# Layer 2's attention output comes out with features on partitions, P is divided before its turns, and layer 0's weights are split in two parts

## The chip, the cores and the metric

The kernel runs on one core of one Trainium2 chip. The metric is the time of the whole program on the device, in microseconds (us). The time before is the median of 3 runs.

## The reference

x is [128 graphs, 64 nodes, 256 features], adj one 64x64 matrix of zeros and ones. Four layers follow each other, each as x = layernorm(x + layer(x)):

- Layer 0, graph attention: h = x W; s1 = h a1 and s2 = h a2 (two columns); e = leaky_relu(s1_i + s2_j) * adj; att = softmax(e); elu(att h + beta h).
- Layer 1: (adj x) W + bias.
- Layer 2, attention with 8 heads of 32: softmax(q k^T / sqrt(32)), masked by adj, times v; then o W_proj + b_proj, and o + layernorm(o) with gamma and beta.
- Layer 3, three gated steps: a = adj h; r = sigmoid(a w4 + h u3), z = sigmoid(a w3 + h u3), hv = tanh(a w5 + (r h) u5), h = (1 - z) h + z hv.

## The kernel before

The 8192 rows are cut into 16 units of 512 rows (8 graphs), in four tiles of 128 rows, two graphs each. Products with weights are taken in three passes of TensorE (L122 to L124): the high part of both operands, and each high with the other's low part. So every operand is copied once by ScalarE (high part, L1440) and once by VectorE (low part, L2217). A "gate group" of layer 3 is six such matmuls with 512 columns.

The layers of different units are interleaved. The body of the loop, i = 1 to 11, holds layer 3 of unit i, layer 2's attention of unit i+1, layer 1 and layer 2's projections of unit i+2, and layer 0 of unit i+3. Around the loop are a fill (units 0 to 2 begin) and a drain. Each engine has its own program: a written list of calls in `body`, `fill` and `drain` (TensorE from L924, ScalarE from L1618, VectorE from L2521), and semaphores order them. Every list is carried out strictly in the order written. SyncE issues the loads of x, the stores, and the swap of V's halves; POOL computes the inverse roots of the normalizations. PSUM is two sets of four banks, X and Y: in the loop layer 3 works in X, and layers 0, 1 and 2 in Y (`front`); for unit 0 `front` is X.

Layer 2's attention of a unit goes so: `l2_mask` and `l2_score` (TensorE) write scores for 4 tiles and 8 heads; VectorE takes the row maximum (`l2_max`, L2367) and subtracts it into `prob` (`l2_shift`, L2377); ScalarE takes exp (`l2_exp`, L1527), not yet divided. TensorE turns P by 16 transposes (`l2_turn_prob`, L797), ScalarE copies the result (`l2_take_prob`). `l2_attend` (L812) is 64 matmuls with the turned P stationary and, as moving operand, 64 columns of V and two columns of ones, so that the row sums of P come out beside the output. VectorE takes the reciprocals of the sums (`l2_inverse`, L2383), adds NaN for rows without a neighbour (`l2_nan`), and multiplies the output by them into `o_tok` (`l2_share`, L2395). The rows are then on partitions, so eight transposes (`l2_turn_o`, through `turn`, L646) bring the features there; `l2_high_o` and `l2_low_o` copy them, and `l2_output` multiplies with W_proj.

In the fill, layer 0's W and its two columns W a1 and W a2 are one matrix of 258 columns. VectorE computes the columns (`sum_a`, four operations), ScalarE takes the high part of all 258 (`high_l0`), VectorE the low part (`low_l0`), and `l0_project` (258 columns for each tile) waits for it. `l0_diagonal` (VectorE), `l0_spread` (TensorE, L698), the softmax on VectorE and ScalarE, `l0_turn_att` (L706) and `l0_attend` (L714) follow. `keep_busy` issues transposes of the identity whose result nobody reads: 38 in the fill.

## Time and profile before

| | |
|---|---|
| median of 3 runs | 1385.81 us (1384.9 to 1387.71) |
| the profiled execution, whole | 1390.11 us |
| its span, first to last instruction | 1388.3 us |
| mean granted TensorE clock | 0.987 |
| instructions | 26972 |
| busy: VectorE / ScalarE / POOL | 1057.0 / 783.7 / 134.2 us |
| the chain that ended last | TensorE 91%, VectorE 6%, ScalarE 2%, issue 1% |

How to read it: a busy share is a mean over the span. Matmuls are pipelined, so that the duration of one (some 400 ns for 512 columns) is longer than the distance to the next (some 235 ns); distances between starts are what counts. PEclk is the granted clock of TensorE, 1.00 for 2.4 GHz and 0.50 for 1.2 GHz; between them a stretch holds both.

### The profile page before, as it was taken

How to read it: one execution, taken by the hardware profiler on the slowest of the kernel's cores; microseconds unless marked ns; L12 is line 12 of the kernel's file. 1: busy time of each engine (PE TensorE's matmuls, PEld its weight loads, DVE VectorE, ACT ScalarE, POOL GpSimd, SP SyncE). 2: the span in 40 equal slices, each digit the busy share in tenths (PEclk: the TensorE clock that was granted, in tenths of full speed). 3: DMA queues.
4: the chain of work that ended last, by engine and by line, in shares of the span. 5: the costliest groups of instructions: out<-in, count | busy, mean ns of one | idle time of the engine just before them, and what ended most of it. 6: DMA issues, size and time to landing. Idle time of an engine off the chain costs nothing.

```text
span 1388.3 us, 26972 instructions
## 1 busy us (share of the span) xinstructions
PE 1345.8 (97%) x10447; PEld 1143.7 (82%) x10447; DVE 1057.0 (76%) x2371; ACT 783.7 (56%) x1449; POOL 134.2 (10%) x194
## 2 busy tenths in 40 slices
PE   7879999999999999999999999999999999999996
PEld 6768888888888888888888888888888888887785
DVE  5776878877787887778787787887778877868465
ACT  3536556656465565656646565664656556564453
POOL 4000101000010100100000010100001010010000
PEclk8979999999999999999999999999999999999998
DMA  5001010000000000000000000000000000010000
GB/s 176 9 1 39 1 24 32 17 13 25 23 30 23 30 15 8 30 23 30 23 30 8 15 30 23 30 15 23 15 23 30 23 31 1 9 38 20 27 1 30
DMA packets 54670, 34.53 MB, mean 25 GB/s; under 512 B 34912, under 2 KB 51552, under 8 KB 54624
## 3 DMA queue, kind: packets, MB, share of 16 engines
q1 hardware_dynamic: 52816, 29.43, 7.1%
q0 software_dynamic: 1248, 3.94, 0.9%
q8 instruction: 31, 0.51, 0.1%
q10 hardware_dynamic: 560, 0.52, 0.1%
q14 instruction: 15, 0.12, 0.0%
HBM read 12.92 MB, written 8.39 MB: 15 GB/s over the span
## 4 chain that ended last, share of the span: by engine, by line
PE 91%; DVE 6%; ACT 2%; issue 1%; DMA 0%; POOL 0%; POOLq 0%; DVEq 0%; ACTq 0%
PE banks L122 22%; PE banks L124 21%; PE banks L123 21%; PE banks L651 8%; PE banks L646 4%; PE banks L812 2%; PE banks L714 2%; PE banks L797 2%; PE banks L914 2%; PE banks L786 2%; PE banks L698 1%; PE banks L775 1%; PE banks L706 1%; DVE l_s L2243 0%; DVE late_lo L2217 0%
## 5 line engine op out<-in xcount | busy, mean ns | idle before, releaser
L1574 ACT ACTIVATE l_r<-banks,bias_r 128x512 f32<-128x512 f32 x90 | 61.5, 683 | 182.3 <-PE banks L124 182.3
L1591 ACT ACTIVATE banks<-banks,bias_h 128x512 f32<-128x512 f32 x96 | 63.5, 662 | 107.0 <-PE banks L124 106.5
L262 POOL TENSOR_TENSOR l_rstd<-l_mv,eps 128x4 f32<-128x4 f32 x47 | 18.3, 389 | 877.2 <-DVE l_mv L256 877.2
L2217 DVE TENSOR_TENSOR l_rh_lo<-l_r,l_rh_hi 128x512 fp32r<-128x512 f32 x90 | 60.7, 687 | 52.9 <-ACT l_rh_hi L1440 51.7
L276 ACT ACTIVATE y<-l_sum,l_offset,l_rstd 128x256 f32<-128x256 f32 x128 | 71.1, 595 | 11.8 <-DVE l_offset L270 11.8
L122 PE MATMUL banks<-l_rh_hi,u_hi 128*128 128x512 f32 x180 | 75.2, 418 | 0.7 <-DVE l_rh_lo L2217 0.7
L1440 ACT ACTIVATE l_rh_hi<-l_r 128x512 fp32r<-128x512 f32 x90 | 54.0, 630 | 36.5 <-DVE l_r L2460 36.5
L1585 ACT ACTIVATE banks<-banks,bias_z 128x512 f32<-128x512 f32 x96 | 62.9, 656 | 17.7 <-PE banks L124 17.7
L124 PE MATMUL banks<-l_rh_lo,u_hi 128*128 128x512 f32 x180 | 71.1, 395 | 0.0
L123 PE MATMUL banks<-l_rh_hi,u_lo 128*128 128x512 f32 x180 | 70.8, 394 | 0.0
L651 PE MATMUL banks<-adj_t,y 128*128 128x128 f32 x544 | 69.5, 277 | 0.5 <-ACT y L276 0.2
L651 PEld LDWEIGHTS banks<-adj_t,y 128*128 128x128 f32 x544 | 64.6, 192 | 4.1 <-issue 3.2
L2478 DVE SCALAR_TENSOR_TENSOR l_r<-banks,l_r 128x512 f32<-128x512 f32 x90 | 61.6, 686 | 5.3 <-ACT banks L1585 2.0
L651 PE MATMUL banks<-adj_t,l_htok 128*128 128x128 f32 x480 | 62.6, 278 | 0.1
L651 PEld LDWEIGHTS banks<-adj_t,l_htok 128*128 128x128 f32 x480 | 57.3, 192 | 6.0 <-ACT l_htok L1440 5.3
L2460 DVE SCALAR_TENSOR_TENSOR l_r<-l_r,l_h 128x512 f32<-128x512 f32 x60 | 40.9, 682 | 26.7 <-ACT l_r L1574 26.7
L1507 ACT ACTIVATE l_qk<-banks 128x512 f32<-128x512 f32 x64 | 38.3, 600 | 40.3 <-PE banks L124 39.8
L2471 DVE TENSOR_TENSOR l_r<-banks,l_h 128x512 f32<-128x512 f32 x60 | 41.1, 685 | 23.4 <-ACT banks L1591 23.3
L2217 DVE TENSOR_TENSOR l_h_lo<-l_h,l_h_hi 128x512 fp32r<-128x512 f32 x60 | 40.9, 682 | 18.1 <-ACT l_h_hi L1440 18.0
L122 PE MATMUL banks<-late_hi,qkv_hi 128*128 128x512 f32 x128 | 51.8, 404 | 2.4 <-DVE late_lo L2217 2.4
L2367 DVE TENSOR_REDUCE l_mx<-banks 128x8 f32<-128x512 f32 x64 | 42.3, 682 | 14.8 <-PE banks L786 14.8
L124 PE MATMUL banks<-late_lo,qkv_hi 128*128 128x512 f32 x128 | 51.6, 403 | 0.0
(304 smaller groups left out, 4331.9 us busy)
## 6 DMA issues: line engine op xcount, KB each, us to landing
x_tok<-in_x_dram SPq DMA_DIRECT2D x15, 512.0 KB, 3.5
l_res<-y SPq DMA_DIRECT2D x15, 512.0 KB, 3.0
out_dram<-l_res SPq DMA_DIRECT2D x15, 512.0 KB, 3.0
l_vpair<-l_vstage SPq DMA_DIRECT2D x32, 128.0 KB, 3.2
w_raw<-in_L_gnn_w_w_dram POOLq DMA_DIRECT2D x3, 512.0 KB, 7.7
qkv_raw<-in_L_gnn_w_qkv_dram POOLq DMA_DIRECT2D x1, 768.0 KB, 4.4
l_res<-in_x_dram SPq DMA_DIRECT2D x1, 512.0 KB, 5.1
u_raw<-in_L_gnn_u_w_dram POOLq DMA_DIRECT2D x2, 256.0 KB, 7.7
```

Of the source, the lines that this page charges most:

```text
L122: nc.tensor.matmul(out, w[0], x[0], start=first, stop=False, skip_group_check=True)
L123: nc.tensor.matmul(out, w[1], x[0], start=False, stop=False, skip_group_check=True)
L124: return nc.tensor.matmul(out, w[0], x[1], start=False, stop=last, skip_group_check=True)
L276: return self.p.nc.scalar.activation(y[:, t, :], z[:, t, :], ACT.Identity, scale=self.rstd[:, t:t + 1], bias=self.offset[:, t:t + 1])
L646: ins = nc.tensor.transpose(bank[:, columns(t)], tokens[:, t, k * P:(k + 1) * P], p.ident[:, :])
L651: ins = nc.tensor.matmul(bank[:, columns(t)], tokens[:, t, k * P:(k + 1) * P], p.adj_t[:, :], start=True, stop=True)
L1440: return nc.scalar.activation(out, source, ACT.Copy)
L1574: nc.scalar.activation(own(u).r[:, m, :], rz(u)[:, m, :], ACT.Tanh, scale=0.5, bias=w.biases["r"][:, m:m + 1]).then_inc(s.r_ready.of(u), 1)
L1585: nc.scalar.activation(rz(u)[:, m, :], rz(u)[:, m, :], ACT.Tanh, scale=0.5, bias=w.biases["z"][:, m:m + 1]).then_inc(s.z_ready.of(u), 1)
L1591: nc.scalar.activation(hv(u)[:, m, :], hv(u)[:, m, :], ACT.Tanh, bias=w.biases["h"][:, m:m + 1]).then_inc(s.hv_ready.of(u), 1)
L2217: return nc.vector.tensor_tensor(parts[1][:, k, :], bank, parts[0][:, k, :].bitcast(F32), ALU.subtract)
L2478: nc.vector.scalar_tensor_tensor(own(u).r[:, m, :], rz(u)[:, m, :], 1.0, own(u).r[:, m, :], ALU.add, ALU.mult).then_inc(s.step.of(u), 1)
```

## The change

Layer 2. VectorE now sums P's rows with four reductions (`l2_sum`), takes the reciprocals and adds NaN as before, and multiplies P by them in place (`l2_normal`), four operations, before the turns; `l2_turn_prob` waits for that. `l2_attend` has its operands exchanged: V is stationary, the turned P moves, and the output has features on partitions, in the layout that `l2_high_o` reads. `l2_turn_o`, `l2_share` and the ones columns are gone (VW is 64 instead of 66).

```diff
         def l2_turn_prob(u, t):
-            pe.wait_ge(*s.l2_exp.at(u, t + 1))
+            pe.wait_ge(*s.l2_prob_shared.at(u, t + 1))
...
         def l2_attend(u, t):
-            pe.wait_ge(*s.l2_prob_t.at(u, t + 1))
-            for g in range(HP):
+            pe.wait_ge(*s.l2_prob_t.at(u, max(t + 1, CH)))
+            for c in range(CH):
                 for n in range(PER_TILE):
-                    at = g * P + n * NODES
-                    ins = nc.tensor.matmul(front(u)[n * NODES:(n + 1) * NODES, t, g * VW:(g + 1) * VW],
-                                           probt[:, t, at:at + NODES], b.v_pair[:, n, t, g, :],
-                                           start=True, stop=True)
+                    for g in range(HP // CH):
+                        at = (c * (HP // CH) + g) * P + n * NODES
+                        ins = nc.tensor.matmul(front(u)[g * VW:(g + 1) * VW, c, t * P + n * NODES:t * P + (n + 1) * NODES],
+                                               b.v_pair[:, n, t, c * (HP // CH) + g, :], probt[:, t, at:at + NODES],
+                                               start=True, stop=True)
...
-        def l2_turn_o(u, k):
-            if k == 0:
-                pe.wait_ge(*s.l2_o.at(u, 1))
-            turn(front(u)[:, k, :], b.o_tok, k).then_inc(s.l2_o_turned.sem, 1)
...
         def l2_high_o(u, k):
-            act.wait_ge(*s.l2_o_turned.at(u, k + 1))
+            act.wait_ge(*s.l2_pv_done.at(u, TILES))
...
+        def l2_sum(u, t):
+            dve.wait_ge(*s.l2_exp.at(u, t + 1))
+            nc.vector.tensor_reduce(b.inv[:, t, :], b.prob[:, t, :, :], AX.X, ALU.add).then_inc(s.l2_inv.sem, 1)
...
+        def l2_normal(u, t):
             if t == 0:
-                dve.wait_ge(*s.l2_inv.at(u, 2))
-            ins = nc.vector.tensor_tensor(b.o_tok[:, t, :].rearrange("p (g e d) -> p g e d", g=HP, e=2),
-                                          heads(u)[:, t, :, 0:2 * HD].rearrange("p g (e d) -> p g e d", e=2),
-                                          b.inv[:, t, :, :].unsqueeze(3).to_broadcast([P, HP, 2, HD]), ALU.mult)
+                dve.wait_ge(*s.l2_inv.at(u, TILES + 2))
+            nc.vector.tensor_tensor(b.prob[:, t, :, :], b.prob[:, t, :, :],
+                                    b.inv[:, t, :].unsqueeze(2).to_broadcast([P, HEADS, NODES]),
+                                    ALU.mult).then_inc(s.l2_prob_shared.sem, 1)
```

Layer 0's weights. W's 256 columns are split by themselves as soon as W has landed; the two s columns are split after `sum_a` (`high_columns`, `low_columns`). For unit 0 the s columns are multiplied separately, 24 matmuls of two columns (`project_columns`), ahead of the projections, and copied by VectorE (`take_columns`). The spread of unit 0 goes to another bank, after the first projection.

```diff
         def high_l0():
+            act.wait_ge(w.loaded[0], 16)
+            nc.scalar.activation(w.l0[0][:, :, 0:DIM], w.l0_raw[:, :, 0:DIM], ACT.Copy).then_inc(ws["l0_hi"], 1)
+
+        def high_columns():
             act.wait_ge(ws["start_chain"], SUMS_OF_A)
-            nc.scalar.activation(w.l0[0][:, :, :], w.l0_raw[:, :, :], ACT.Copy).then_inc(ws["l0_hi"], 1)
+            nc.scalar.activation(w.l0[0][:, :, DIM:WX], w.l0_raw[:, :, DIM:WX], ACT.Copy).then_inc(ws["columns_hi"], 1)
...
+        def project_columns():
+
+            pe.wait_ge(ws["columns_ready"], 1)
+            pe.wait_ge(*s.l0_lo.at(0, CH))
+            for t in range(TILES):
+                ins = rows_by_weights(s_columns[:, t, :], b.early, t, w.l0, slice(DIM, WX))
+            ins.then_inc(ws["l0_columns"], 1)
```

Unit 0's three first normalizations are applied half by ScalarE (tiles 0, 1) and half by VectorE (tiles 2, 3). The orders of all engines are rewritten. In the loop's body TensorE's order between the scores and the output, where calls that are the same on both sides stand once, is now:

```diff
             l2_mask(i + 1)
-            l3_w(i, 0, 0)
             l2_score(i + 1, 0)
...
             l3_u(i, 0, 0)
             l3_u(i, 0, 1)
             l3_r(i, 0, 0)
+            l3_w(i, 0, 0)
+            l3_w(i, 0, 1)
             l3_r(i, 0, 1)
-            l3_w(i, 0, 1)
+            l3_diff(i, 0, 0)
             l2_turn_prob(i + 1, 0)
...
             l2_attend(i + 1, 3)
-            l3_diff(i, 0, 0)
             l3_candidate(i, 0, 0)
-            l2_turn_o(i + 1, 0)
-            l2_turn_o(i + 1, 1)
             l3_candidate(i, 0, 1)
             l3_diff(i, 0, 1)
             l2_output(i + 1, 0)
```

And VectorE's there:

```diff
             l2_shift(i + 1, 3)
+            l3_variance(i - 1)
             l3_reset(i, 0, 0)
+            l2_sum(i + 1, 0)
+            l2_sum(i + 1, 1)
+            l2_sum(i + 1, 2)
+            l2_sum(i + 1, 3)
+            l2_inverse(i + 1)
+            l3_offset(i - 1)
+            l2_nan(i + 1)
+            l2_normal(i + 1, 0)
+            l2_normal(i + 1, 1)
+            l2_normal(i + 1, 2)
+            l2_normal(i + 1, 3)
             l3_reset(i, 0, 1)
-            l3_variance(i - 1)
             l3_low_rh(i, 0, 0)
             l3_low_rh(i, 0, 1)
-            l2_inverse(i + 1)
-            l2_nan(i + 1)
-            l2_share(i + 1, 0)
-            l2_share(i + 1, 1)
-            l2_share(i + 1, 2)
-            l2_share(i + 1, 3)
+            l2_low_o(i + 1, 0)
             l3_difference(i, 0, 0)
-            l2_low_o(i + 1, 0)
```

On ScalarE the fourth exponential now stands ahead of the second reset, and the second r*h copy ahead of the fourth copy of P. In the fill `keep_busy` has 159 transposes at 16 places instead of 38 at four; the projections of unit 2 stand ahead of unit 0's turns of P. In the drain layer 3's `l3_diff` stands earlier.

## Rows read from the trace of the kernel before

**Rows 1.** The page, part 1: busy time, share of the span, instructions.
```profile
PE 1345.8 (97%) x10447; PEld 1143.7 (82%) x10447; DVE 1057.0 (76%) x2371; ACT 783.7 (56%) x1449; POOL 134.2 (10%) x194
```

**Rows 2.** Windows: stretch, its length, busy time of each engine, PEclk, DMA share.
```profile
12.40:17.00 4.60, 4.52 (x24) 4.44 (x24) 2.13 (x15) 1.16 (x3) 4.60 (x7) 0.63 0.94 195
24.90:30.60 5.70, 5.62 (x20) 4.91 (x21) 3.25 (x5) 2.93 (x5) 0.00 (x0) 0.55 0.01 3
71.00:80.40 9.40, 6.84 (x92) 6.23 (x90) 6.41 (x19) 5.33 (x10) 1.21 (x2) 0.82 0.01 2
85.00:105.00 20.00, 14.31 (x56) 11.11 (x56) 17.49 (x48) 6.03 (x12) 2.46 (x4) 0.66 0.00 1
0.00:105.00 105.00, 80.88 (x648) 70.22 (x649) 73.72 (x184) 44.33 (x84) 23.12 (x44) 0.87 0.20 62
...
544.50:626.80 82.30, 82.21 (x647) 70.09 (x647) 65.02 (x146) 48.37 (x90) 7.45 (x10) 1.00 0.07 22
1250.00:1388.30 138.30, 122.91 (x676) 101.05 (x674) 86.65 (x179) 63.40 (x110) 7.50 (x12) 0.96 0.05 20
```

**Rows 3.** Timeline of TensorE in one loop turn: start, duration, instruction.
```profile
612.95 0.50 PE L122 MATMUL banks<-f_h_hi,u_hi 128*128 128x512 f32 x1
...
620.06 1.91 PE L797 MATMUL banks<-ident,l_prob 128*128 128x128 f32 x16
621.90 2.10 PE L812 MATMUL banks<-l_vpair,l_qk 128*64 128x66 f32 x64
623.92 0.50 PE L122 MATMUL banks<-f_a_hi,diff_hi 128*128 128x512 f32 x1
...
626.83 1.03 PE L646 MATMUL banks<-ident,l_otok 128*128 128x128 f32 x8
627.62 0.47 PE L122 MATMUL banks<-l_rh_hi,u_hi 128*128 128x512 f32 x1
...
628.39 0.39 PE L122 MATMUL banks<-l_rh_hi,u_hi 128*128 128x512 f32 x1
...
629.08 0.39 PE L122 MATMUL banks<-f_a_hi,diff_hi 128*128 128x512 f32 x1
```

**Rows 4.** Groups of VectorE: count, busy us and mean ns, idle before.
```profile
L2367 DVE TENSOR_REDUCE l_mx<-banks 128x8 f32<-128x512 f32 x64 | 42.3, 682 | 14.8 <-PE banks L786 14.8
L2377 DVE TENSOR_TENSOR l_prob<-banks,l_mx 128x512 f32<-128x512 f32 x64 | 42.0, 679 | 0.1
...
L2395 DVE TENSOR_TENSOR l_otok<-banks,l_inv 128x256 f32<-128x256 f32 x64 | 22.7, 416 | 0.5
...
L2383 DVE RECIPROCAL l_inv<-banks 128x32 f32<-128x32 f32 x16 | 5.6, 352 | 7.0 <-PE banks L812 7.0
```

**Rows 5.** Timeline of VectorE in the same loop turn.
```profile
613.01 1.29 DVE L2367 TENSOR_REDUCE l_mx<-banks 128x8 f32<-128x512 f32 x2 [1.22 <-PE banks L786]
...
616.61 1.27 DVE L2377 TENSOR_TENSOR l_prob<-banks,l_mx 128x512 f32<-128x512 f32 x2
```

**Rows 6.** Timeline of ScalarE in the same loop turn.
```profile
617.46 0.69 ACT L1574 ACTIVATE l_r<-banks,bias_r 128x512 f32<-128x512 f32 x1 [8.33 <-PE banks L124]
618.04 1.66 ACT L1527 ACTIVATE l_prob<-l_prob 128x512 f32<-128x512 f32 x3
```

**Rows 7.** Timeline of TensorE in the fill; in brackets the idle time before and its releaser.
```profile
12.48 0.39 PE L122 MATMUL banks<-l_w_hi,early_hi 128*128 128x258 f32 x1 [1.97 <-DVE l_w_lo L2157]
...
18.15 0.67 PE L698 MATMUL banks<-l_s,same_graph 128*128 128x256 f32 x2 [1.03 <-DVE l_s L2243]
...
24.98 3.78 PE L714 MATMUL banks<-l_h,l_att_t 128*128 128x256 f32 x8 [0.69 <-ACT l_att_t L1440]
...
38.27 2.05 PE L651 MATMUL banks<-adj_t,y 128*128 128x128 f32 x16 [0.22 <-ACT y L276]
...
115.99 0.47 PE L122 MATMUL banks<-f_h_hi,u_hi 128*128 128x512 f32 x1
```

**Rows 8.** Timeline of TensorE in the drain.
```profile
1290.45 1.09 PE L914 MATMUL banks<-ident,l_h 128*128 128x128 f32 x8 [2.30 <-DVE l_h L2484]
```

1552 lines of the change are left out of this document (801 added, 751 removed).

## The prediction

> **What bounds the kernel now.** I read the page first: TensorE is busy for 97% of the span, VectorE for 76% [rows 1]. A mean hides stages, so I took windows. One turn of the loop lasts 82.3 us and TensorE is busy for 82.21 of them at full clock, VectorE for 65.02; the first 105 us are another regime, with 24.1 us in which TensorE does nothing (105.0 - 80.88) and a mean granted clock of 0.87; the last 138.3 us hold 15.4 us of idleness [rows 2]. So in the loop a TensorE instruction that goes is time that goes, unless a new wait takes its place, and VectorE has 17 us of air per unit. In the fill what counts is the chain of hand-overs, and whether the clock is at 2.4 or 1.2 GHz when the work comes. In four stretches of it the clock stands at 0.63, 0.55, 0.82 and 0.66; busy time by missing clock is 4.52 x 0.37 + 5.62 x 0.45 + 6.84 x 0.18 + 14.31 x 0.34 = 10.3 us that the same columns would not need at full clock [rows 2].
>
> The sum is made against the profiled execution, 1390.1 us with a span of 1388.3. It is 4.3 us above the median of 1385.8; I take the difference found onto the median.
>
> **1. The output's turns go.** Eight 128x128 transposes a unit. In the loop they start at 626.83 and the next matmul at 627.62, 0.79 us; the three passes after it take 0.77 instead of the 0.69 of the next ones, which is the price of going back from these small transposes to the long matmuls [rows 3]. 0.79 + 0.07 = 0.86 us a unit, all of it on the engine that bounds, 16 units: -13.8 us. In the fill, where TensorE also idles, part of this is only air; I count that in step 5.
>
> **2. The attention matmuls with operands swapped.** 64 a unit, before and after. Before, P is stationary and V moves in 66 columns (the two ones columns give the row sums); after, V is stationary and P moves in 64. They take from 621.90 to 623.92, 2.02 us [rows 3], 32 ns each. If streaming sets the pace, 2 of 66 columns are 0.06 us a unit; if loading 64 stationary columns does, nothing. Consecutive instructions still go to alternate halves of the columns. Between 0 and -1.0 us for 16 units; I take -0.5, the middle. The Trainium skill (TensorEngine Tiling (Array Packing), Key Properties) says that changing the tiling mode drains TensorE; both versions switch into and out of this mode once a unit, so the 0.07 us above stays paid here and the rule changes nothing but the warning that splitting blocks costs.
>
> **3. More switches.** The new body splits two blocks of small matmuls (layer 1's second aggregation, layer 2's second input turn) and joins one (mask and scores): about half a switch more per unit, between 0 and 0.15 us each way. I take +0.04 a unit, +0.6 us in all.
>
> **4. VectorE ahead of P's turns.** It gets four row sums over 128x512 and four multiplications of 128x512, and loses four 128x256 shares. Nearest rows: the row maximum (a reduction of the same size, from PSUM) 682 ns, the subtraction in P 679, share 416, reciprocal 352, and the NaN add, which is no longer than that [rows 4]. In sequence they start every 0.6 us (two maxima take 1.29 together [rows 5]). So VectorE gets 8 x 0.6 - 4 x 0.36 = 3.4 us a unit, 65 to 68.4 of some 81: it fits by throughput. Neither operation is seen with both ends in SBUF; bounds 0.5 and 0.9 us each.
>
> By latency: let 0 be the start of the first l3_u after the scores, 612.95. Before, the path to P's turns was: four maxima, four shifts (end 617.88, 4.93), ScalarE's reset from 617.46 (4.51), four exponentials at 5.09, 5.61, 6.13 and (now without the reset between) 6.65 [rows 5, 6]; TensorE reached the turns at 620.06, 7.11, after five gate groups of 1.41 us [rows 3]. The new order puts seven groups there: 9.95. VectorE in the new order: shifts to 4.9, layer 3's variance 0.4, reset 5.2 to 5.9, sums at 5.9, 6.5, 7.1, 7.7 (the last waits for the last exponential, done 7.3), reciprocal 8.4, NaN add 8.8, multiplications from 9.05 every 0.6, ending 9.7, 10.3, 10.9, 11.5. TensorE's four groups of turns (0.46 each, 1.84 from 620.06 to 621.90) are there at 9.95, 10.41, 10.87, 11.33. The last is late by 0.2 us. The first attention group now waits for two copies of P, and ScalarE does layer 3's second r*h copy before the last P copy; by the same addition that copy ends near 13.6 and its group is due at 13.7. Candidate 0 needs both low parts of r*h, ready at 13.8 against 14.2. Then 4.2 us of candidates and gates lie over o's high and low copies (2 x 0.6 + 0.7, with a tanh between them). So the cover just holds everywhere. A stall of 0.2 us by this addition; with each of the eight new operations 0.1 longer than the 0.6 it is 1.0. I take 0.24 a unit for the 14 units from the loop on: +3.3 us. Layer 3's second r*h is queued behind the multiplications; it is the next to be late.
>
> A rule speaks against the change: the Trainium skill (VectorE: DVE Perf Modes, Rules for kernel authors) calls tensor_reduce the slowest VectorE operation and says to restructure where it is on a hot path, and here sums that came from ones columns become reductions. The trace does not bear it out for this size: the maximum takes 682 ns and a tensor_tensor 679 [rows 4]. By that rule alone the sums would be late, which is case D below.
>
> **5. The fill.** Before, four sum operations and a split of the whole W stand ahead of the first projection, which starts at 12.48 after 1.97 us idle, and the spread of s2 waits for all four projections, copies and diagonal: 18.15 [rows 7]. After, W's 256 columns are split at once and the two s columns by themselves: 24 matmuls of two columns before the projections, 0.7 to 2.4 us (24 x 0.032 of step 2, or x 0.10 of the turns), I take 1.5; the diagonal follows without the 4.5 us of projections at half speed. Spread at about 14, 4 us earlier. The first attend (3.78 us for 8 matmuls at half clock, 24.98 [rows 7]) takes half of that if the clock is kept. Half of the tiles of unit 0's three normalizations go to VectorE, which shortens each by some 1.0 us (two of four ScalarE applications); that is on the chain that ends at 38.27 with the first aggregation [rows 7]. Against it: unit 0's P is now divided with no layer 3 to cover it, 8 x 0.6 + 0.6 - 1.4 (shares) = 4.0 us; four projections of unit 2 (2.9 us) are moved over it. The filler transposes rise from 38 to 159, 121 more by 0.10 = 12 us of TensorE time; they cost nothing while they lie in the 24 us of idleness, and all of the 12 if that idleness has gone. Their use is the 10.3 us of missing clock. Sum: at best -4 - 3 - 10.3 + 2 = about -15; at worst the clock is not kept and fillers get in the way, +4. I take -8, nearer to the best end, since I can follow the chain to the spread and to the first attend and these alone give -6. POOL now sums the biases before unit 0's root, so that root waits for the last weight load; that is hidden unless the loads end later than that root is due, 6 us before its old place at the earliest. The issues on SP (unit 3's x before the keeping of y2 of unit 0) have no taker near.
>
> **6. The drain.** Its orders are new. The 2.30 us wait for h before a turn at 1290 [rows 8] should shrink, as the gates are issued earlier; unit 15's division has gates over it. Between -3 and +3; I take 0.
>
> Sum: -13.8 - 0.5 + 0.6 + 3.3 - 8 = -18.4 us: 1371.7 of the profiled execution, 1367.4 on the median; I say **1367**.
>
> **Cases.**
> A (0.58). As summed, 1367, its own range 1361 to 1374.
> B (0.12). No stall in the loop and the fill at its best end: 1367.4 - 3.3 - 5 = 1359. For it: the loop before has 0.1 us of idleness in 82, and the new order gives exactly two more gate groups as cover.
> C (0.15). The fill gives nothing because its chain, not TensorE, sets the pace and the fillers only fill: 1375. For it: in 85 to 105 us VectorE is busy for 17.49 of 20 [rows 2]. Against: the clock there is 0.66.
> D (0.08). Eight new operations at 0.7 or the sums late: stall 1.0 a unit, 14 - 3.3 = 11 more: 1378.
> E (0.07), slower. P's turns wait fully: if sums and multiplications run after the last exponential and layer 3's reset and r*h queue between them, the last multiplication ends near 14 instead of 11.5, a stall of 2.6 us at every unit: 1367.4 - 3.3 + 14 x 2.6 = 1400. It decides from a stall of (18.4 + 3.3) / 14 = 1.55 us a unit. Against it: the order interleaves the sums with the exponentials.
> That the change does not do what it says would show in 128 transposes still there; the diff leaves no caller, I give it nothing.
>
> 0.2% or 2.8 us is what a measurement tells from no change. Faster: all of A, B, C, D less a rest, 0.90; same 0.03; slower 0.07. The range runs from B's to just above D's time, 1357 to 1380; C and D are each at the other end of a cost that I could only bound.
>
> **What would show it.** Right: no group of transposes on the output tile; the loop's period 81.4 to 81.7 instead of 82.3; idle before P's turns, put down to VectorE's multiplication, under 0.3 us in each loop turn; the multiplication and the sum at 0.6 to 0.7 us; the spread near 14, the first l3_u of unit 0 at 106 to 109 instead of 115.99 [rows 7], and a granted clock above 0.95 in the first 105 us. Wrong: a period of 82.3 or more (step 4), the clock still near 0.87 (step 5), or waits of the u5 matmuls for r*h's low part in each loop turn.

## The result and the profile after

| | before | after |
|---|---|---|
| median beside each other on one chip | 1387.44 us (8 runs) | 1381.68 us (8 runs) |
| ratio | | 0.9958, 95% interval 0.9945 to 0.9971 |
| the profiled execution, its span | 1388.3 us | 1380.3 us |

The change makes the kernel faster by 0.42%, 5.8 us, and by 8.0 us between the two profiled executions. 18.4 were forecast. 1381.7 lies above the range of 1357 to 1380.

The page, part 1, of the kernel after, against [rows 1]:

```profile
PE 1350.2 (98%) x10464; PEld 1143.7 (83%) x10464; DVE 1109.4 (80%) x2441; ACT 796.3 (58%) x1444; POOL 138.2 (10%) x194
```

128 transposes are gone, 121 idle ones and 24 matmuls of two columns have come (17 instructions more), and TensorE is busy for 4.4 us longer: a matmul that waits in the middle of its group is shown as busy. A busy sum doesn't answer the question. The windows, against [rows 2], say a little more (length, PE, PEld, DVE, ACT, POOL, clock, DMA):

```profile
0.00:105.00 105.00, 95.93 (x850) 87.19 (x850) 81.92 (x202) 49.55 (x95) 25.39 (x44) 0.97 0.24 73
...
544.50:626.80 82.30, 82.17 (x643) 69.46 (x642) 68.45 (x152) 50.12 (x92) 7.63 (x10) 1.00 0.07 22
1250.00:1380.30 130.30, 115.00 (x629) 94.97 (x627) 80.02 (x166) 58.48 (x102) 7.29 (x12) 0.95 0.06 21
```

In the first 105 us the granted clock went from 0.87 to 0.97, as step 5 wanted. In the loop VectorE has 3.4 us more of work, as step 4 had it.

What does answer it is a mark that every unit passes. The mask of a unit is the first matmul of its attention; here are the masks of units 1, 2, 3 and 13 and the last group of TensorE. Before:

```profile
113.71 0.61 PE L775 MATMUL banks<-mask_bias,ident_bf 64*128 64x512 bf16 x4
...
197.07 0.61 PE L775 MATMUL banks<-mask_bias,ident_bf 64*128 64x512 bf16 x4
...
280.15 0.61 PE L775 MATMUL banks<-mask_bias,ident_bf 64*128 64x512 bf16 x4
...
1102.72 0.61 PE L775 MATMUL banks<-mask_bias,ident_bf 64*128 64x512 bf16 x4
...
1377.38 1.14 PE L914 MATMUL banks<-ident,x_tok 128*128 128x128 f32 x8 [2.20 <-DVE x_tok L2484]
```

After:

```profile
103.50 0.60 PE L804 MATMUL banks<-mask_bias,ident_bf 64*128 64x512 bf16 x4
...
187.82 0.61 PE L804 MATMUL banks<-mask_bias,ident_bf 64*128 64x512 bf16 x4
...
273.33 0.83 PE L804 MATMUL banks<-mask_bias,ident_bf 64*128 64x512 bf16 x4
...
1094.10 0.61 PE L804 MATMUL banks<-mask_bias,ident_bf 64*128 64x512 bf16 x4
...
1369.93 1.48 PE L937 MATMUL banks<-ident,x_tok 128*128 128x128 f32 x8 [2.32 <-DVE x_tok L2524]
```

After minus before: -10.2, -9.2, -6.8, -8.6, -7.4 us. So the fill (all that lies ahead of the loop) gives all that it was to give (unit 1), 3.4 us are lost again between units 1 and 3 (1.0 up to unit 2, in the last part of the fill, and 2.4 behind it), ten turns of the loop give 1.8 together, 0.18 each, and the drain takes 1.2. The period is (1094.10 - 273.33) / 10 = 82.08 us, against 82.26; 81.4 to 81.7 was forecast.

**One loop turn.** TensorE, against [rows 3]:

```profile
613.39 0.40 PE L124 MATMUL banks<-f_a_lo,diff_hi 128*128 128x512 f32 x1
613.62 2.46 PE L826 MATMUL banks<-ident,l_prob 128*128 128x128 f32 x16
616.01 2.08 PE L841 MATMUL banks<-l_qk,l_vpair 128*64 128x64 f32 x64
618.03 0.50 PE L122 MATMUL banks<-l_rh_hi,u_hi 128*128 128x512 f32 x1
```

P's turns took 1.84 us from their first start to the start of the attend, and take 2.39 in this turn (2.34 in the mean); no idle time stands before them, because TensorE waits between the groups of four, inside the row. VectorE in the same turn:

```profile
606.45 2.47 DVE L2413 TENSOR_TENSOR l_prob<-banks,l_mx 128x512 f32<-128x512 f32 x4
...
609.14 0.65 DVE L2500 SCALAR_TENSOR_TENSOR l_r<-l_r,f_h 128x512 f32<-128x512 f32 x1
609.72 2.46 DVE L2419 TENSOR_REDUCE l_inv<-l_prob 128x8 f32<-128x512 f32 x4
612.21 0.35 DVE L2424 RECIPROCAL l_inv<-l_inv 128x32 f32<-128x32 f32 x1
612.48 0.10 DVE L272 SCALAR_TENSOR_TENSOR l_offset<-l_mv,l_rstd 128x4 f32<-128x4 f32 x1
612.60 0.24 DVE L2430 TENSOR_SCALAR l_inv<-l_inv,nan_rows 128x32 f32<-128x32 f32 x1
612.87 2.50 DVE L2437 TENSOR_TENSOR l_prob<-l_prob,l_inv 128x512 f32<-128x512 f32 x4
```

The first multiplication ends at about 613.5, just when TensorE is through with its gates, and the other three follow at 0.6 us. TensorE needs 0.46 for a group, so it runs at VectorE's pace: its groups of four start at 613.62, 614.22, 614.82 and 615.43. The groups of VectorE, against [rows 4]:

```profile
L2413 DVE TENSOR_TENSOR l_prob<-banks,l_mx 128x512 f32<-128x512 f32 x64 | 40.0, 678 | 0.0
L2437 DVE TENSOR_TENSOR l_prob<-l_prob,l_inv 128x512 f32<-128x512 f32 x64 | 40.0, 686 | 0.5
L2419 DVE TENSOR_REDUCE l_inv<-l_prob 128x8 f32<-128x512 f32 x64 | 39.7, 675 | 0.4 <-ACT l_prob L1558 0.2
```

The new operations cost 675 and 686 ns, within the bounds of 0.5 and 0.9, and the sum is no slower than the subtraction.

**The loop's entry.** TensorE at unit 2, in the first turn of the loop:

```profile
187.82 0.61 PE L804 MATMUL banks<-mask_bias,ident_bf 64*128 64x512 bf16 x4
188.36 1.56 PE L815 MATMUL banks<-l_qk 32*64 32x64 f32 x125
191.67 0.33 PE L815 MATMUL banks<-l_qk 32*64 32x64 f32 x3 [1.75 <-issue]
...
193.44 0.63 PE L124 MATMUL banks<-f_h_lo,u_hi 128*128 128x512 f32 x1
193.87 0.63 PE L122 MATMUL banks<-f_h_hi,u_hi 128*128 128x512 f32 x1
```

Three matmuls from its end, the block of 128 short score matmuls stands still for 1.75 us, and nothing that the profile shows is waited for ("issue"). A microsecond later matmuls come every 0.43 us instead of 0.235 for some 3.4 us: the granted clock there is 0.50, 1.2 GHz. Before, the same block stood still for 0.51 us and the clock stayed at 1.00. 1.75 - 0.51 plus seven distances longer by 0.196 is 2.6 us, which covers the 2.4 lost between the masks of units 2 and 3.

**The same fill in six traces.** There is a second trace of the kernel after (e15 below), and e5, e6, e7 and e9 have its fill and change the loop alone. In these six traces the mask of unit 1 comes at 101.8 to 102.0 us where the clock stays at 1.00 in the first 105 us (e5, e6, e15) and at 103.5 to 103.8 where it falls for 3.4 or 6.8 us (after, e7, e9). A difference of 2 us at unit 1 between single traces can so be the clock of one execution and nothing of the kernel.

### The profile page after: what moved, and what is told of

Its sections match the earlier page's. It is cut to its first block, busy times and chain, and to the rows that moved or that the text cites. A ratio compares the mean times of both kernels' runs of the same rounds, so it can differ in the third digit from the quotient of the medians.

```text
span 1380.3 us, 27146 instructions
## 1 busy us (share of the span) xinstructions
PE 1350.2 (98%) x10464; PEld 1143.7 (83%) x10464; DVE 1109.4 (80%) x2441; ACT 796.3 (58%) x1444; POOL 138.2 (10%) x194
## 4 chain that ended last, share of the span: by engine, by line
PE 91%; DVE 5%; ACT 2%; issue 1%; DMA 0%; POOL 0%; SPq 0%; POOLq 0%; ACTq 0%; DVEq 0%
PE banks L122 23%; PE banks L124 22%; PE banks L123 22%; PE banks L667 9%; PE banks L662 3%; PE banks L937 2%; PE banks L826 2%; PE banks L841 2%; PE banks L743 2%; PE banks L815 2%; PE banks L725 1%; PE banks L804 1%; PE banks L656 1%; PE banks L735 0%; DVE early_lo L2249 0%
## 5 line engine op out<-in xcount | busy, mean ns | idle before, releaser
L2249 DVE TENSOR_TENSOR early_lo<-banks,early_hi 128x512 fp32r<-128x512 f32 x62 | 41.8, 685 | 36.1 <-ACT early_hi L1469 35.8
L278 ACT ACTIVATE y<-l_sum,l_offset,l_rstd 128x256 f32<-128x256 f32 x124 | 68.2, 593 | 2.8 <-DVE l_offset L272 2.7
L1469 ACT ACTIVATE late_hi<-banks 128x512 fp32r<-128x512 f32 x66 | 39.1, 597 | 38.6 <-PE banks L662 23.1
```

The lines of the kernel that those rows point to most:

```text
L278: return self.p.nc.scalar.activation(y[:, t, :], z[:, t, :], ACT.Identity, scale=self.rstd[:, t:t + 1], bias=self.offset[:, t:t + 1])
L1469: return nc.scalar.activation(out, source, ACT.Copy)
L2249: return nc.vector.tensor_tensor(parts[1][:, k, :], bank, parts[0][:, k, :].bitcast(F32), ALU.subtract)
```

## The experiments

"Before" ran beside each set: 1387.0, 1387.7, 1386.9, 1387.6 and 1386.1 us, for e1 to e4, e5 to e8, e9 and e10, e11 to e13, and e14 and e15.

### VectorE's pace: less work for it (e1)

This kernel leaves the row sums out, so that P is divided by 1.

```diff
-            nc.vector.tensor_reduce(b.inv[:, t, :], b.prob[:, t, :, :], AX.X, ALU.add).then_inc(s.l2_inv.sem, 1)
+            nc.vector.memset(b.inv[:, t, :], 1.0).then_inc(s.l2_inv.sem, 1)
```

> The changed kernel with the four row sums per unit (2.46 us of VectorE) replaced by four small memsets, so P is divided by 1: the division's chain is some 2.2 us shorter and nothing else changes. Theory V (VectorE's pace in the chain sums, reciprocal, NaN, multiplications sets when P's turns end): the block of 16 turns falls from 2.34 us back to 1.84 as before the change, the loop's period from 82.08 to about 81.55, the time by 11 x 0.5 plus 1 to 2 us in fill and drain, to about 1375. Rival T (the turns cost more on TensorE itself, because each group now waits by itself or because of the stretch around it): block and period stay, the time stays within 1.5 us of 1381.7. The drain's wait for h of unit 14 (3.7 us) should shrink only if VectorE's load for unit 15 makes it: about 2.4 us less VectorE work ahead of it, so 1.3 to 2.4 us under that theory, unchanged if it is the chain of layer 3 itself.

Measured: 1376.15 us, ratio 0.9923 (0.9902 to 0.9945). TensorE in the same turn:

```profile
612.12 1.91 PE L826 MATMUL banks<-ident,l_prob 128*128 128x128 f32 x16
613.99 2.09 PE L841 MATMUL banks<-l_qk,l_vpair 128*64 128x64 f32 x64
```

The turns are back at 1.87 us in every loop turn, and the period is 81.70 us against 82.08. Nothing of TensorE was changed, so what stretched them is VectorE's lateness, worth 0.38 us a turn, and 5.1 to 5.5 us of the kernel (10.9 us under its "before" where the kernel after is 5.8 under its own; 1376.15 against 1381.68). The stall at the entry (1.90 us) and the drain's wait for h (3.6 us) stayed: they have other causes.

### The fourth multiplication on POOL (e3)

```diff
+            nc.gpsimd.tensor_tensor(b.prob[:, t, :, :], b.prob[:, t, :, :],
+                                    b.inv[:, t, :].unsqueeze(2).to_broadcast([P, HEADS, NODES]),
+                                    ALU.mult).then_inc(s.l2_last_shared.sem, 1)      # t = TILES - 1, POOL's list
```

> The changed kernel with the fourth of the four multiplications of P moved from VectorE to POOL, beside the other three. VectorE's chain gets 0.6 us shorter. Theory V: if POOL's multiplication of 128x512 takes up to 2.0 us, it ends when the last turn needs it, the block of turns falls from 2.34 to about 1.9, the period to about 81.65, the time to about 1376. If it takes over 2.5 us, the fourth group of turns waits for it and the block grows by what it is over: at 4 us some 2 us a unit, 1405. Rival T: with a POOL time under 2 us nothing moves. No row so far shows a POOL operation of this size but a memset of 0.53 us; tensor_tensor of 4 elements takes 0.33 to 0.55.

Measured: 1389.97 us, ratio 1.0026 (1.0012 to 1.0040), period 82.77. The groups, VectorE and then POOL:

```profile
L2457 DVE TENSOR_TENSOR l_prob<-l_prob,l_inv 128x512 f32<-128x512 f32 x48 | 44.0, 967 | 0.5
...
L593 POOL TENSOR_TENSOR l_prob<-l_prob,l_inv 128x512 f32<-128x512 f32 x16 | 24.7, 1542 | 93.5 <-DVE l_inv L2448 93.5
```

The mean of 967 ns mixes two sizes. VectorE's three and POOL's one in the same turn:

```profile
614.23 0.69 DVE L2457 TENSOR_TENSOR l_prob<-l_prob,l_inv 128x512 f32<-128x512 f32 x1
614.84 1.53 DVE L2457 TENSOR_TENSOR l_prob<-l_prob,l_inv 128x512 f32<-128x512 f32 x1
616.29 0.68 DVE L2457 TENSOR_TENSOR l_prob<-l_prob,l_inv 128x512 f32<-128x512 f32 x1
...
614.27 1.55 POOL L593 TENSOR_TENSOR l_prob<-l_prob,l_inv 128x512 f32<-128x512 f32 x1 [1.98 <-DVE l_inv L2448]
```

One of the three, in every unit, takes 1.53 us and the other two keep their 0.69 and 0.68; the long one begins while POOL's is under way and ends after it. Together they take 2.74 us, more than four at 0.6, and the second group of turns waits for the long one (0.80 us). The help costs more than it saves. The Trainium skill (SBUF — State Buffer, Who interferes with whom) says that a VectorE instruction with two inputs in SBUF contends with a GpSimd instruction that reads SBUF. The trace agrees, with 0.84 us on one VectorE instruction in each unit and nothing on the others.

### The fill: idle transposes, halves, order

```diff
e2: keep_busy 12, 5, 3 and 18 at the places of the kernel before, the other groups out (159 -> 38)
e4: unit 0's three normalizations, t = 2 and 3: VectorE's calls out, ScalarE's loops over range(4)
e10, TensorE's fill:
-            project_columns()
             l0_turn(1, 1)
...
-            l0_spread(0)
             for n in range(1, 4):
                 l0_project(0, n)
+            project_columns()
+            l0_spread(0)
```

> The changed kernel with the filler transposes of the fill cut from 159 to 38, at the places where the old kernel had them (12, 5, 3, 18). Theory K (the fill's gain of 10 us is to a good part kept clock): the mean granted clock of the first 105 us falls from 0.97 towards the old 0.87, the mask of unit 1 comes 4 to 7 us later, and the time goes up by as much, to 1386 to 1389. Rival C (the gain is the shorter chain alone, fillers only fill idleness): the clock falls but the mask of unit 1 moves by less than 1.5 us and the time stays within 1.5 us of 1381.7. Rival W (fillers are in the way): 2 to 4 us faster.

> The changed kernel with unit 0's three normalizations applied by ScalarE alone again (four tiles each), VectorE's three pairs taken out. If these applications are on the fill's chain, each of the three ends some 1.0 us later and the mask of unit 1 comes 2 to 3 us later, the time goes up by 2 to 3 us to 1384 to 1385. Rival: other work covers them, the time stays within 1 us.

> The changed kernel with the attention's two columns of unit 0 (project_columns) and l0_spread(0) behind the four projections of unit 0 in TensorE's fill, as in the kernel before, and not ahead of them; the weights stay in two parts. It prices the order that the weights in two parts allow. Theory K2 (it is the head of the fill's chain): VectorE's scores of unit 0, which begin at 17.5 in the changed kernel, begin 3 us later, the mask of unit 0 comes 2.5 to 3 us later, that of unit 1 too, and the end 2 to 3: 1384. Rival (the fill's chain goes through the loads and the weights of the layers behind, so the head's 3 us are absorbed by the waits between): masks of units 0 and 1 within 1 us, and 1382.

| | median, ratio | mask of unit 1 | unit 2 | unit 3 |
|---|---|---|---|---|
| after | 1381.68, 0.9958 | 103.50 | 187.82 | 273.33 |
| e2 | 1382.85, 0.9970 (0.9955 to 0.9985) | 106.83 | 192.04 | 273.92 |
| e4 | 1383.59, 0.9979 (0.9965 to 0.9993) | 106.35 | 190.15 | 274.06 |
| e10 | 1383.75, 0.9981 (0.9969 to 0.9993) | 105.12 | 189.51 | 273.19 |

Without its part unit 1 comes later by 3.3 us (e2), 2.9 (e4) and 1.6 (e10). By the scatter of 2 us between traces of the same fill, e2 and e4 are clear of it, and e10 isn't: what the order of the columns is worth is not shown. Theory K wanted 4 to 7 us for the idle transposes and is near with 3.3; the halves were priced at 2 to 3 and came so. At unit 3 all stand within 0.9 us of each other, and the whole times differ by 1 to 2 us, hardly more than the intervals. It looks as if the entry took whatever the fill gained, but the traces say otherwise: from unit 2 to unit 3 the kernel after needs 85.5 us, e4 83.9 and e10 83.7, each with a stall in unit 2's scores (1.75, 1.75 and 1.46 us) and only the first with a fall of the clock behind it, and e2 needs 81.9 and has no stall there (it has one of 1.14 us earlier, in unit 1's scores). The entry differs by kernel, and hides what the fill is worth; e14 below, with the idle transposes and no stall at the entry, has unit 3's mask 5.2 us ahead of e2's (268.76 against 273.92), of which 0.7 is the difference of their stalls in unit 1's scores. The fill was tried from the other side too, with the old order and more idle transposes (e8):

```diff
 # the kernel before, TensorE's fill: 38 -> 111
+            keep_busy(20)                    # behind l1_product(1)
+            keep_busy(14)                    # and 8 behind it, around l0_turn_att(2)
+            keep_busy(8)                     # and 12 behind it, around l2_turn(1)
+            keep_busy(11)                    # ahead of f_turn(0)
```

> The kernel BEFORE with 73 more idle transposes on TensorE in its fill (20 behind l1_product(1), 14 and 8 around l0_turn_att(2), 8 and 12 around l2_turn(1), 11 ahead of f_turn(0)), nothing else. It prices the granted clock apart from the rest of the fill's change. Theory K (the fill's gain is mostly the clock): the 13.7 us at half clock from 91.4 go, 3.4 of 74.3 too, unit 1's mask comes 5 to 7 us earlier than in the kernel before, and the end by 3 to 6: 1382. Theory W (the gain is mostly the weights in two parts and the earlier first product): unit 1's mask comes 1 to 3 us earlier at most. The entry of the loop may give some of it back, as it did where unit 1 was early in the changed kernel; if the giving back belongs to a unit that is early at all, the gap closes by about 3 us between the masks of units 1 and 3 here too; if it belongs to the scores directly behind the mask, it does not, since this kernel has a product between them.

Measured: 1385.55 us, ratio 0.9981 (0.9963 to 1.0000); masks of units 1, 2 and 3 at 109.41, 192.73 and 275.01, 4.3, 4.3 and 5.1 us earlier than before, and the last group 3.1. The 13.7 us at half clock from 91.4 on are gone. The clock alone is about 4 of the fill's 10 us, and in this order nothing is lost at the entry. From unit 13's mask to the last group this kernel needs 276.43 us where the kernel before needs 274.66 with the same instructions; step 6 below comes back to these 1.8 us.

### What stands behind the mask (e5)

```diff
             l2_mask(i + 1)
+            l3_w(i, 0, 0)
             l2_score(i + 1, 0)
...
             l3_r(i, 0, 0)
-            l3_w(i, 0, 0)
```

> The changed kernel, in TensorE's loop body alone, with the product l3_w(i,0,0) back where the kernel before has it, between the mask and the scores, instead of behind l3_r(i,0,0). Theory F (the stall at the loop's entry comes from the scores' 128 short instructions directly behind the mask, for which instructions must be fetched): the idle time of 1.75 us put down to issue inside the first loop turn's scores goes to under 1 us, no stretch at half clock follows it, and the mask of unit 3 comes 2 to 3 us earlier than in the changed kernel, while the masks of units 1 and 2 stay. Theory V (VectorE's chain max, shift, sum, inverse, normalize starts at the scores and paces the turns of P): the scores now come 1.4 us later and so does all of VectorE's chain, with 1.41 us less TensorE work as cover; the block of P's turns grows by 1.2 to 1.4 us in each loop turn, to about 3.6, the period by as much, to 83.3, and the whole kernel by some 13 x 1.3 = 17 us less the 2.5 of the entry, to about 1396. Rival T (the turns of P are slow by themselves): the block stays at 2.3 and the time falls to about 1379.

Measured: 1394.62 us, ratio 1.0051 (1.0034 to 1.0069), period 83.55. TensorE at unit 2, at unit 3 and in a later turn:

```profile
188.36 1.93 PE L815 MATMUL banks<-l_qk 32*64 32x64 f32 x128
...
270.04 0.66 PE L804 MATMUL banks<-mask_bias,ident_bf 64*128 64x512 bf16 x4
...
617.68 2.46 PE L826 MATMUL banks<-ident,l_prob 128*128 128x128 f32 x16 [1.07 <-DVE l_prob L2437]
```

Both halves came out. The scores run through (x128 in one row), there is no half clock, and the first loop turn takes 83.81 us where the later ones take 83.55; in the kernel after it is 85.50 against 82.08. (Unit 3's mask is 3.3 us earlier than after, but 1.6 of them are there at unit 2 already.) In every later turn the chain that starts at the scores is 1.4 us later, its cover a product shorter, and the loss goes one to one into the period: 1.47 us. This is the margin of the new order from both sides: no time is left in it for anything ahead of P.

### Three orders that try to gain the half microsecond

```diff
e6, TensorE:
+            l2_attend(i + 1, 0)
             l2_turn_prob(i + 1, 3)
-            l2_attend(i + 1, 0)
e7, VectorE: l3_variance(i - 1) behind l3_low_rh(i, 0, 1); l3_offset(i - 1) ahead of l3_gated(i, 0, 1)
    ScalarE: l3_apply(i - 1, 0..1) behind l3_high(i, 0, 0), (2..3) behind l1_high(i + 2, 1)
e9, as e7 with l3_offset behind l2_low_o(i + 1, 0), and
    ScalarE: l3_reset(i, 0, 0) behind l2_exp(i + 1, 3); VectorE: l3_reset(i, 0, 0) behind l2_inverse(i + 1)
```

> The changed kernel, in TensorE's loop body alone, with the first attend group ahead of the fourth group of P's turns. Theory V: the groups of turns are 0.60 us apart because VectorE makes one product in 0.60, and TensorE needs 0.46 for one; the first attend group's 0.50 us then lies in the time in which the fourth product is made, so the fourth group's wait of 0.14 goes, and the copies that ScalarE makes of the first groups may bring a small wait of their own before the first attend: period lower by 0.1 to 0.2 us, the kernel by 1 to 2 us, 1380. Rival (two more changes from turns to attend and back cost 0.1 to 0.2 and the copy of the second group is not there yet): no change or slower by 1 to 2 us.

> The changed kernel, in the loop bodies of VectorE and ScalarE alone: the variance and offset of layer 3's norm of the unit before, 0.28 and 0.10 us of VectorE ahead of the sums and the normalizing of P, go behind l3_low_rh and l3_difference of step 0, and ScalarE's four l3_apply behind them with it. Theory V: the four products of P are done 0.4 us earlier, TensorE reaches P's turns at the same time, and its waits there (0.50 a unit) nearly vanish: the block of P's turns from 2.34 to 1.9, the period from 82.08 to 81.65, the kernel by 13 x 0.43 = 5 to 6 us, to about 1376. Rival T2 (the gain returns as a wait of layer 3's h or of y, since l3_apply now lies in ScalarE's queue between l3_high and l3_take_h): P's turns shrink all the same but the period stays within 0.1 of 82.08.

> The changed kernel, in the loop bodies of ScalarE and VectorE alone. ScalarE makes the four exponentials of P ahead of layer 3's tanh of r (m=0) and not behind it; VectorE makes the product r times h (m=0) behind the inverse of the sums and not ahead of the sums; layer 3's variance goes behind l3_low_rh, its offset behind l2_low_o(0), and ScalarE's four l3_apply behind them. Theory V, as the trace of the run with the share early leaves it: ScalarE begins the exponentials at 608.67 there, 1.9 us after the first shifted tile is there, because its tanh waits for TensorE's r at 607.96; so VectorE's sums cannot begin before 609.3. With the exponentials first the sums follow the shifts at once, 0.7 us earlier, and the products of P are done 0.4 to 0.7 us earlier against TensorE: three of four lie ready when TensorE comes. The block of P's turns goes from 2.34 to 1.85 to 1.95, the period from 82.08 to 81.6, the kernel by 12 x 0.45 = 5 us: 1376 to 1377. Rival T2 (the other link: what TensorE needs next, rh_lo for the candidate, is not there earlier, so the time saved at P's turns comes back as a wait before l3_candidate or for h): P's turns shrink to 1.9 but the period stays above 81.9.

e6: 1386.06 us, ratio 0.9983 (0.9968 to 0.9997), period 82.47. The attend waited 0.18 us for a copy of P; that the two more changes of tile shape cost the rest is likely and was not measured by itself. The rival was right. e7: 1381.62 us, ratio 0.9960 (0.9941 to 0.9979), period 82.05, 0.03 shorter; the turns 2.25 in the mean instead of 2.34. Theory V was wrong by a factor of four in the size of that, and the period stayed, as rival T2 had it: in the trace after, the offset at 612.48 starts before the reciprocal's result can be used, and the variance ends while ScalarE still makes its first exponential. They stood in gaps that stay when they go. e9 made it plain; it is slower than after, 1384.91 us, ratio 0.9987 (0.9975 to 0.9999), period 82.42. VectorE there:

```profile
611.85 2.46 DVE L2419 TENSOR_REDUCE l_inv<-l_prob 128x8 f32<-128x512 f32 x4 [0.70 <-ACT l_prob L1558]
```

I had read the four shifts as one for each exponential. Each shift is a group of rows over all four tiles, so the first exponential needs all four (it starts when the last shift ends), and the moved product of r and h had filled exactly the 0.7 us of that exponential. From the scores to P's turns the chain is tight: 2.4 maxima, 2.4 shifts, an exponential, 2.4 sums, 0.7 for the inverse, and 0.6 for each multiplication.

### The place of the stall at the entry

```diff
e11: 18 -> 5, and the groups of 4, 14, 4, 4, 10, 4, 5 and 9 ahead of unit 0's l2_turn out (159 -> 92)
e12: keep_busy 12 -> 15 ahead of l0_turn(0), 18 -> 25 behind it (159 -> 169); e14 is e12 again
e13: 18 -> 5, and the groups of 4, 4, 4 and 5 out (159 -> 129)
e15: the kernel after again
```

> The changed kernel with 67 of the 159 idle transposes of its fill left out, all ahead of unit 0's second layer (13 of the 18, the 4, 14, 4, 4, 10, 4, 5 and 9); the 75 behind unit 1's l1_product stay. Theory F2: the stall of 1.75 us at the loop's entry stands at the 126th of the scores' 128 short instructions because the next piece of the loop's instructions begins there, and it shows only where short instructions leave TensorE no work in hand; the place moves with the number of instructions ahead of the loop, by one matmul later for each one left out. So here it lies 67 matmuls later, behind 42 long ones and the 16 turns of P, at the start of the attends, which are short again: a stall there of up to 1.7 us or none. Theory G (the stall comes from the clock or from how early a unit is, as unit 1's mask at 103.5): it stays inside the scores if unit 1's mask stays at 103 to 105. Both: the late transposes keep the clock, so the half clock at 70 and 94 of the kernel with few of them stays away, and the end comes 0 to 2 us earlier than in the changed kernel, at 1380 to 1382.

> The changed kernel with ten more idle transposes at its start (15 for 12 ahead of l0_turn(0), 25 for 18 behind it). Theory F2: the stall at the loop's entry moves ten matmuls earlier, to about the 116th of unit 2's scores, and stays at 1.5 to 1.8 us; the masks of units 0 and 1 are within 1 us of the changed kernel's. Theory G: it stays at the 126th.

> The changed kernel with 30 of the 159 idle transposes of its fill left out (13 of the 18 and the four groups 4, 4, 4 and 5), the others where they are. Theory F2: the next piece of the loop's instructions begins 30 matmuls later, 27 behind the scores, among the 42 matmuls of 512 columns, where TensorE has work in hand: no idle time over 0.5 us put down to issue at the entry and no half clock behind it; the distance from unit 2's mask to unit 3's goes from 85.5 to 82.3, and if the clock holds in the fill without the thirty (masks of unit 1 at 103.5 to 104.5) the kernel ends 2 to 3.2 us earlier: 1378.5 to 1380. Theory G: the distance stays at 84.5 to 85.5 and the time at 1382.

> The kernel of e12 again (the changed kernel with ten more idle transposes at its start), timed over more rounds beside the changed kernel. If the stall at the loop's entry is what the ten transposes take away, and nothing else differs: 1377.5 to 1379, 3 to 4.5 us under the changed kernel, and again no idle time over 0.5 us in unit 2's scores.

> The changed kernel itself once more, on the same chip as e14. Its stall at the 126th of unit 2's scores (1.75 us) is expected again in the same place, if it belongs to where the instructions lie and not to chance, and its time at 1381 to 1383.

| | median | ratio to before | units 2 to 3 | stall at unit 2 |
|---|---|---|---|---|
| e11 | 1378.95 (5 runs) | 0.9937 (0.9922 to 0.9952) | 81.9 | none |
| e12 | 1377.89 (2 runs) | 0.9932 (0.9911 to 0.9954) | 81.9 | none |
| e13 | 1382.49 (11 runs) | 0.9965 (0.9954 to 0.9977) | 81.9 | none |
| e14 | 1378.17 (6 runs) | 0.9943 (0.9923 to 0.9963) | 81.9 | none |
| e15 | 1380.79 (9 runs) | 0.9954 (0.9937 to 0.9970) | 85.5 | 1.79, at the same matmul |

The masks of units 1, 2, 3 and 13 in e14:

```profile
102.21 0.60 PE L804 MATMUL banks<-mask_bias,ident_bf 64*128 64x512 bf16 x4
...
186.82 0.61 PE L804 MATMUL banks<-mask_bias,ident_bf 64*128 64x512 bf16 x4
...
268.76 0.60 PE L804 MATMUL banks<-mask_bias,ident_bf 64*128 64x512 bf16 x4
...
1089.53 0.61 PE L804 MATMUL banks<-mask_bias,ident_bf 64*128 64x512 bf16 x4
```

Theory G falls: unit 1 comes at 102 to 105 in all five, and only the kernel with 159 idle transposes stalls, twice in the same place. So do all others with 159 and the scores directly behind the mask: e1, e3, e6, e7, e9 and e10 stall at the same 126th matmul, for 1.46 to 1.92 us. e4 has 159 too, but four waits fewer in TensorE's fill; it stalls for 1.75 us at the 128th score matmul and not at the 126th. Two matmuls are four instructions (each has a load of weights), so there the place moved as F2 says. But F2 holds only in part. The stall does depend on how many instructions stand ahead of the loop and goes where thirty fewer stand there. But ten more did not move it ten matmuls earlier: it is gone from unit 2's scores, and a smaller one has come in unit 1's, a unit earlier (0.66 us in e12, 0.48 in e14); my picture of one border that shifts with the count is wrong. The trace shows the fetches of instructions as packets of 16 KB on a queue of their own: in the kernel after two of them stand 4.3 us apart at the entry, at 188.9 and 193.2 us, in e14 one already lies at 182.6, ahead of the loop, and the next at 189.4 and 202.7. The stall begins while the first of the close pair is under way (188.9 to 190.4) and ends at 191.67. That TensorE waits for such a packet is argued from these times and from the count; the profile names no releaser. The Trainium skill (Runtime: NRT & Kernel Launch, Instruction fetch mechanics) says that crossing a 16 KiB border is mostly hidden, and that a taken branch can force a fetch before execution continues; the trace agrees with the first, with 32 such packets in the kernel after and one stall over 0.4 us, and whether the loop's branch has a part in it no run here shows. The one place costs 1.75 us, and 3.6 with the clock behind it (85.5 against 81.9).

The same can happen elsewhere. e13 lost nothing at the entry, but from unit 13's mask to the last group it needs 3.7 us more than e12, and so missed its forecast of 1378.5 to 1380. 2.6 of them are this row in the scores of unit 15 and another stall of 1.2 put down to issue; the clock is also low for 6.8 us there and not for 3.4:

```profile
1238.02 0.36 PE L815 MATMUL banks<-l_qk 32*64 32x64 f32 x11 [1.40 <-issue]
```

e14 is the best version that ran: 2.6 us under the kernel after on the same chip (1378.17 against 1380.79; both with intervals of some 0.2%, so that the medians alone would not carry it, but the 3.6 us between the masks of units 2 and 3 do, in four traces against two).

## Why the prediction was wrong

The step that failed is the fourth: the wait of TensorE at P's turns was put at 0.24 us a unit and is 0.50. Beside it stand the entry of the loop, 3.4 us that no step had, and in step 3 a wait for y, 0.26 us a turn, that was left out.

By its own steps, per unit in the loop; measured is the distance from a group's first matmul to the next group's, meaned over the turns from unit 3 to unit 12.

| step | predicted | measured |
|---|---|---|
| 1, output's turns | -0.86 | -0.79, and -0.07 of the switch |
| 2, attend | -0.03 | -0.01 |
| 3, switches and the rest | +0.04 | +0.19 |
| 4, P's turns | +0.24 | +0.50 |
| sum | -0.61 | -0.18 |

**Step 1** was right. **Step 2** was right in that it is nearly nothing.

**Step 3** was mis-sized, and by a wait and not by the switches. TensorE around f_turn, the first transposes of y of layer 2:

```profile
642.17 0.40 PE L124 MATMUL banks<-l_a_lo,w5s_hi 128*128 128x512 f32 x1
642.63 0.66 PE L662 MATMUL banks<-ident,y 128*128 128x128 f32 x4
```

f_turn starts 0.44 us behind the last product's start in the mean, and did 0.23 before; the copy of y on ScalarE ends at 642.58, so it waits for y. Its own first distance grew from 0.11 to 0.17. Together this is 0.26 a turn, more than the whole 0.19. Without it the matmuls of 512 columns fell by 0.10, of which the switch that went is 0.07, and the small groups come to -0.04 in all: the new splits have no price that shows. That f_turn would wait appears nowhere in the prediction: I followed o and h behind the change, and not y.

**Step 4** failed in its size, and it is the loop's main error. Its places were nearly right: counted from the first l3_u (603.72 in the turn shown), TensorE reaches P's turns at 9.90 where 9.95 was said, and VectorE multiplies from 9.15 to 11.65 where 9.05 to 11.5 was said. The addition took the ends of the four multiplications (9.7, 10.3, 10.9, 11.5) and called only the last late, by 0.2. A tenth or two later at the front, all but the first are late, and the last group of turns starts at 615.43 in place of 613.62 + 3 x 0.46 = 615.00: 0.43 late. It then takes 0.58 to the first attend matmul and not 0.46, since a group that had to wait starts slowly (0.17 between its first two transposes and 0.11 between the others): together 0.55 in this turn, 0.50 in the mean. The margin was zero: VectorE delivers a group every 0.6 us and TensorE takes one every 0.46, so that the last group is late by three times the difference as soon as the first is not early, and an error of 0.15 in a chain of 11 us doubled the stall. The bounds that I gave, 0.2 and 1.0, hold the 0.50; case D's story (slow operations) did not happen.

**Step 5** was right in sum: unit 1 is 10.2 us earlier where 9.7 was said (8 and the turns), 11.7 in e15, where the clock held. Its clock was said to be above 0.95 and is 0.97. Its parts fit less well: the spread starts at 16.44 and not near 14, 1.7 us earlier than before where 4 were said, and the first aggregation at 34.14, 4.1 us earlier.

**What no step had** is the entry of the loop: 3.4 us lost where two turns were to give 1.2, 2.4 of them in the first turn of the loop. [rows 2 to 4] are all from settled turns and from the fill; no row was read from 190 to 205 us, where the kernel before already had its 0.51 us of issue. Had the instructions lain as in e14, the time would have been 1378, inside the range, and step 4 would still be wrong.

**Step 6** was put at 0 within -3 to +3; measured +1.2 from unit 13's mask to the last group, while its two units were to give 1.2 from steps 1 to 4. The wait that was to shrink grew [rows 8]:

```profile
1281.41 1.70 PE L937 MATMUL banks<-ident,l_h 128*128 128x128 f32 x8 [3.56 <-DVE l_h L2524]
```

3.56 us against 2.30. It stayed at 3.6 without the sums (e1), so the new VectorE work is not its cause; that leaves the new order of the drain, where all of unit 14's gates stand ahead of its candidates and none is left to lie over VectorE's work behind them. No run here undid that order, so this is argued and not shown. But the wait is not the larger part of the loss. Right behind it the clock is low for 3.4 us, in the kernel after and, behind a wait of 2.29 us, in e8, which has the kernel before's drain; in the kernel before it is not (windows of after, e8 and before: length, PE, PEld, DVE, ACT, POOL, clock, DMA):

```profile
1281.70:1285.10 3.40, 3.40 (x19) 3.40 (x18) 0.00 (x0) 1.96 (x5) 0.00 (x0) 0.51 0.38 154
...
1286.60:1290.00 3.40, 3.40 (x19) 3.40 (x18) 0.69 (x1) 1.57 (x4) 0.00 (x0) 0.50 0.38 154
...
1290.40:1296.00 5.60, 5.55 (x49) 5.42 (x49) 1.55 (x3) 3.46 (x7) 0.00 (x0) 1.00 0.23 94
```

From unit 13's mask to the last group e8 needs 1.8 us more than the kernel before, with the same instructions and the same waits. So some 1.8 of the 2.4 us that are missing in the drain are the clock of this stretch, and the one trace of the kernel before was lucky in it: against e8 the new drain is 0.6 us shorter.

Of 11 us missing up to the last group, then: 4.6 between units 1 and 3, 4.3 in the ten turns, and 2.4 in the drain, less 0.5 that the fill gave beyond its forecast.

## What to carry to other kernels

When work is moved from the engine that bounds to one with air, price the whole chain between two marks of the bound engine, and compare the pace of producer and consumer: if they meet at the first piece and the producer is slower per piece, the difference is paid on every piece behind it. Before an instruction is moved "off the chain", look at what it lies beside: one that stands in another's latency gives nothing when it goes, and takes time when it comes back elsewhere. Read the first turn of a loop as a stretch of its own, before and after: where short instructions stand there, the place of the code alone can be worth 3 us, and a difference of that size is no verdict on a change of the schedule. And before a difference of 2 us between two traces is put down to a change, look for a stretch at half clock in one of them: two traces of the same fill or drain differed by as much here.

## What was not expected of the hardware

- A stall on TensorE without a wait, in blocks of short matmuls: 1.46 to 1.92 us in the first turn of the loop in nine traces with the same count of instructions ahead of it (four fewer in e4), gone from there by ten transposes more (0.24 us each at most) at the start of the program or thirty fewer, and then 0.5 to 1.4 us elsewhere. In five of the nine the granted clock fell to 1.2 GHz about a microsecond behind it (after, e1, e6, e9, e15), in four it did not (e3, e4, e7, e10).
- One POOL multiplication of 128x512 at 1542 ns stretches one VectorE multiplication that begins beside it from 0.69 to 1.53 us, and leaves the other two as they were.
- A row sum of 128x512 from SBUF, 675 ns, costs as much as an elementwise subtraction from PSUM, 678.
- Behind a wait of 2.3 us in the drain the clock stayed in one trace and fell for 3.4 us in another, with the same instructions; the fall cost 1.8 us.
